# Merging the third and fourth key tile of a head into one exponential, and one masking product for two heads

## What is computed

```
x = x + attention(wkv(x, fside, fside, w1, u1, cond), w_qkv, w_o)
x = x + ffn(wkv(x, fside, fside, w2, u2, cond), w_gate, w_up, w_down)
```

## Time and profile before

| | |
|---|---|
| median of 3 runs | 988.72 us (987.49 to 988.75) |
| the profiled execution | 986.6 us, span 984.6 us |
| PE, matmuls | 728.8 us busy, 74% of the span |
| DVE | 785.0 us, 80% |
| ACT | 473.8 us, 48% |
| ACT's exponentials of attention (L499) | 256, 99.9 us |
| PE's key scores (L1198, L1199, L1200) | 3 x 256 products |
| PE's masks by query (L1176) | 256 products |
| granted TensorE clock, mean | 0.948 |

### The profile page before, as it was taken

One profiled execution on the slowest core, in us unless ns is written; L12 is line 12 of the kernel. 1 busy time (PEld: TensorE's weight loads), 2 busy tenths in 40 slices (PEclk: granted clock), 3 DMA queues, 4 the chain that ended last, 5 costly groups with the idle time before them and its releaser, 6 DMA issues.

```text
span 984.6 us, 10348 instructions
## 1 busy us (share of the span) xinstructions
PE 728.8 (74%) x3761; PEld 361.3 (37%) x3761; DVE 785.0 (80%) x1064; ACT 473.8 (48%) x758; POOL 73.6 (7%) x149
## 2 busy tenths in 40 slices
PE   0110107769878999897889998978899989987656
PEld 0000003334544444444444444444444444653222
DVE  3999999977997878879978788799787886534566
ACT  5645644336675353356753532567535324452230
POOL 1000000111100001111000011110000111100000
PEclk9999999799899999999979999999899998999788
DMA  8612210254400002744000027440000273400001
GB/s 319 235 43 96 96 53 11 66 126 128 109 22 22 1 12 61 206 130 106 22 22 1 11 52 211 124 116 23 22 0 11 53 204 73 100 1 1 1 0 43
DMA packets 30305, 72.23 MB, mean 73 GB/s; under 512 B 5808, under 2 KB 5808, under 8 KB 28464
## 3 DMA queue, kind: packets, MB, share of 16 engines
q1 hardware_dynamic: 19792, 46.94, 15.9%
q0 software_dynamic: 6144, 16.79, 7.2%
q10 hardware_dynamic: 4320, 7.87, 2.3%
HBM read 33.82 MB, written 4.19 MB: 39 GB/s over the span
## 4 chain that ended last, share of the span: by engine, by line
PE 45%; DVE 33%; issue 10%; ACT 8%; DMA 3%; SPq 1%; POOL 0%; DVEq 0%; ACTq 0%
PE bank L1285 12%; PE bank L1148 6%; PE bank L1297 5%; PE bank L1225 4%; PE bank L1214 4%; PE bank L1141 4%; PE bank L1198 4%; ACT region L499 3%; PE bank L1174 3%; DVE negmax L953 2%; DMA stacks<-rows 2%; PE bank L1199 2%; DVE num L853 2%; DVE region L772 2%; DVE fn L839 2%
## 5 line engine op out<-in xcount | busy, mean ns | idle before, releaser
L953 DVE TENSOR_REDUCE negmax<-bank 128x4 f32<-128x512 f32 (+2 forms) x96 | 99.3, 1035 | 52.3 <-PE bank L1176 52.3
L1198 PE MATMUL bank<-stacks 128*128 128x512 f32 (+3 forms) x256 | 108.7, 426 | 35.1 <-ACT region L499 32.2
L499 ACT ACTIVATE region<-bank 128x512 f32<-128x512 f32 (+3 forms) x256 | 99.9, 433 | 64.3 <-PE bank L1200 64.1
L296 POOL DMA_DIRECT2D stacks<-rows x128 | 69.5, 550 | 780.4 <-DVE region L741 361.2
L1148 PE MATMUL bank<-h,wqkv 128*128 128x512 f32 x256 | 116.1, 604 | 7.4 <-DVE region L1105 4.2
L1174 PE MATMUL bank<-stacks 128*128 128x128 f32 (+3 forms) x256 | 85.2, 414 | 9.0 <-DVE negmax L953 4.7
L1199 PE MATMUL bank<-maxrow,pick 128*128 128x512 bf16 (+3 forms) x256 | 83.6, 326 | 0.0
L1141 PE MATMUL bank<-wqkv,h 128*128 128x512 f32 x128 | 70.1, 705 | 16.0 <-ACT rows L487 16.0
L1198 PEld LDWEIGHTS bank<-stacks 128*128 128x128 f32 x256 | 51.5, 201 | 67.2 <-ACT region L499 51.9
L1307 PE MATMUL bank<-identb,region 128*128 128x128 bf16 x36 | 5.5, 307 | 95.3 <-DVE region L749 63.6
L1285 PE MATMUL bank<-region,gate_q 128*128 128x512 bf16 x256 | 62.2, 387 | 16.8 <-DVE region L741 16.8
(11 more groups left out here) (150 smaller groups left out, 1378.8 us busy)
## 6 DMA issues: line engine op xcount, KB each, us to landing
stacks<-rows SPq DMA_DIRECT2D x128, 128.0 KB, 4.0
stacks<-rows POOLq DMA_DIRECT2D x128, 128.0 KB, 4.3
kt<-in_fside ACTq DMA_DIRECT2D x30, 256.0 KB, 3.1
h<-in_x SPq DMA_DIRECT2D x4, 1024.0 KB, 5.7
region<-in_w_gate SPq DMA_DIRECT2D x4, 1024.0 KB, 12.1
xt<-in_x SPq DMA_DIRECT2D x4, 1024.0 KB, 7.3
region<-in_w_up SPq DMA_DIRECT2D x4, 1024.0 KB, 5.5
region<-in_w_down SPq DMA_DIRECT2D x4, 1024.0 KB, 4.6
```

The source lines that it names most:

```text
L296: eng.dma_start(stacks[HD * r:HD * r + HD, at:at + 2, i, :].bitcast(F32), rows[mine, q:k + 1:k - q, :]).then_inc(stacked[s][i], 16)
L499: nc.scalar.activation(probs[:, i, P_AT[t]:P_AT[t] + CAUSAL[t]], bank[4 + n % 2][:, 0:CAUSAL[t]], ACT.Exp, scale=SCALE).then_inc(p_ready, 1)
L953: nc.vector.tensor_reduce(o, scored, AX_X, ALU.max, negate=True).then_inc(max_taken, 1)
L1198: nc.tensor.matmul(o, ks[s][:, i, P * t:P * t + P], qs[s][:, i, P * t:T], start=True, stop=False)
```

## The change

Key tiles 2 and 3 of a head (256 and 128 columns) go into one bank side by side, as one unit with six products and one exponential of 384 columns. A group has 12 units instead of 16. In `scores`, the first two query tiles, where two heads share a bank, get one masking product for both: `hide_qk` is read twice by a step of zero, and the output is two strips of 128 columns. The unit numbers in ACT's order, in the waits of the stacks and in `SLOT_BEHIND` are put in the new count.

```diff
+    KEY_TILES = ((0,), (1,), (2, 3))
+    PER_HEAD = len(KEY_TILES)
+    UNITS = HG * PER_HEAD
...
                 if g >= 2:
-                    eng.wait_ge(st_ready, b * (GROUPS * UNITS) + (g - 2) * UNITS + TT * (i + 1))
+                    eng.wait_ge(st_ready, b * (GROUPS * UNITS) + (g - 2) * UNITS + PER_HEAD * (i + 1))
...
-                    nc.scalar.activation(probs[:, i, P_AT[t]:P_AT[t] + CAUSAL[t]],
-                                         bank[4 + n % 2][:, 0:CAUSAL[t]], ACT.Exp,
+                    nc.scalar.activation(probs[:, i, P_AT[tiles[0]]:P_AT[tiles[0]] + columns],
+                                         bank[4 + n % 2][:, 0:columns], ACT.Exp,
                                          scale=SCALE).then_inc(p_ready, 1)
...
-                exps(b, 0, 0, 6)
+                exps(b, 0, 0, 5)
                 cap_exp(b, 4)
-                exps(b, 0, 6, 10)
+                exps(b, 0, 5, 8)
                 load_k(b, 3)
                 reciprocals(b, 3)
                 own_exp(b, 4)
-                exps(b, 0, 10, 16)
+                exps(b, 0, 8, 12)
...
-                    mm = nc.tensor.matmul(o[:, c + P * t:c + w], identb[:, :], hide_qk[:, :],
-                                          start=False, stop=True, skip_group_check=True)
+                    if t >= 2:
+                        mm = nc.tensor.matmul(o[:, P * t:w], identb[:, :], hide_qk[:, :],
+                                              start=False, stop=True, skip_group_check=True)
+                    elif i % 2:
+                        pair = o[:, 0:2 * w].rearrange("p (i w) -> p i w", i=2)[:, :, P * t:w]
+                        mm = nc.tensor.matmul(pair, identb[:, :], hide_qk[:, :].rearrange("p (o w) -> p o w", o=1).to_broadcast([P, 2, P]),
+                                              start=False, stop=True, skip_group_check=True)
...
-                o = bank[4 + n % 2][:, 0:CAUSAL[t]]
-                nc.tensor.matmul(o, ks[s][:, i, P * t:P * t + P], qs[s][:, i, P * t:T], start=True, stop=False)
-                nc.tensor.matmul(o, pick[:, i, :], maxrow[:, s, P * t:T], start=False, stop=False)
-                nc.tensor.matmul(o[:, 0:P], identb[:, :], hide_kq[:, :], start=False, stop=True).then_inc(st_ready, 1)
+                for t in tiles:
+                    c = P_AT[t] - P_AT[tiles[0]]
+                    o = bank[4 + n % 2][:, c:c + CAUSAL[t]]
+                    nc.tensor.matmul(o, ks[s][:, i, P * t:P * t + P], qs[s][:, i, P * t:T],
+                                     start=True, stop=False, skip_group_check=True)
+                    nc.tensor.matmul(o, pick[:, i, :], maxrow[:, s, P * t:T], start=False, stop=False, skip_group_check=True)
+                    mm = nc.tensor.matmul(o[:, 0:P], identb[:, :], hide_kq[:, :], start=False, stop=True, skip_group_check=True)
+                mm.then_inc(st_ready, 1)
...
-                        if g == 0 and n == 9:
+                        if g == 0 and n == 7:
                             project_values(b, 1)
...
-SLOT_BEHIND = ({1: 0, 3: 1, 6: 2, 9: 3, 12: 4, 15: 5}, {3: 2, 7: 3, 11: 4, 15: 5})
+SLOT_BEHIND = ({1: 0, 2: 1, 4: 2, 7: 3, 9: 4, 11: 5}, {2: 2, 5: 3, 8: 4, 11: 5})
```

More of the change, by code:

```diff
@@ L56, in adaln_attention_ffn @@
     P_LEN = sum(CAUSAL)
-    UNITS = HG * TT
+    KEY_TILES = ((0,), (1,), (2, 3))
+    PER_HEAD = len(KEY_TILES)
+    UNITS = HG * PER_HEAD
     SLOTS = 6
@@ L496, in exps @@
                 for n in range(first, last):
-                    i, t = n // TT, n % TT
+                    i, tiles = n // PER_HEAD, KEY_TILES[n % PER_HEAD]
+                    columns = sum(CAUSAL[t] for t in tiles)
                     act.wait_ge(st_ready, b * (GROUPS * UNITS) + g * UNITS + n + 1)
-                    nc.scalar.activation(probs[:, i, P_AT[t]:P_AT[t] + CAUSAL[t]],
-                                         bank[4 + n % 2][:, 0:CAUSAL[t]], ACT.Exp,
+                    nc.scalar.activation(probs[:, i, P_AT[tiles[0]]:P_AT[tiles[0]] + columns],
+                                         bank[4 + n % 2][:, 0:columns], ACT.Exp,
                                          scale=SCALE).then_inc(p_ready, 1)
@@ L548, in turn @@
                 sum_reciprocal(b, 0)
-                exps(b, 1, 0, 4)
+                exps(b, 1, 0, 3)
                 load_k(b, 4)
@@ L553, in turn @@
                 own_exp(b, 5)
-                exps(b, 1, 4, 12)
+                exps(b, 1, 3, 9)
                 weigh(b, 5, 0)
                 weigh(b, 5, 1)
-                exps(b, 1, 12, 16)
+                exps(b, 1, 9, 12)
                 cap_exp(b, 6)
@@ L563, in turn @@
                 sum_reciprocal(b, 1)
-                exps(b, 2, 0, 4)
+                exps(b, 2, 0, 3)
                 weigh(b, 6, 0)
                 weigh(b, 6, 1)
-                exps(b, 2, 4, 12)
+                exps(b, 2, 3, 9)
                 cap_exp(b, 7)
-                exps(b, 2, 12, 16)
+                exps(b, 2, 9, 12)
                 load_k(b, 6)
@@ L578, in turn @@
                 weigh(b, 7, 1)
-                exps(b, 3, 0, 6)
+                exps(b, 3, 0, 5)
                 cap_exp(b, 8)
-                exps(b, 3, 6, 12)
+                exps(b, 3, 5, 9)
                 load_k(b, 7)
@@ L584, in turn @@
                 own_exp(b, 8)
-                exps(b, 3, 12, 16)
+                exps(b, 3, 9, 12)
                 weigh(b, 8, 0)
@@ L1188, in scores_by_key @@
             def scores_by_key(b, g, n):
-                s, i, t = g % 2, n // TT, n % TT
+                s, i, tiles = g % 2, n // PER_HEAD, KEY_TILES[n % PER_HEAD]
                 if n == 0:
```

## The result

| | before | after |
|---|---|---|
| median | 988.25 us (987.49 to 988.75, 4 runs) | 977.40 us (976.17 to 978.02, 4 runs) |
| ratio | 1 | 0.9889, 95% interval 0.9872 to 0.9906 |
| the profiled execution | 986.6 us, span 984.6 | 977.25 us, span 975.5 |
| granted TensorE clock, mean | 0.948 | 0.955 |

The change wins 10.85 us. A second measurement of the same kernel at another time gave 978.34 us against 989.08, ratio 0.9893 (0.9878 to 0.9909).

What follows compares the result with a forecast made beforehand. PE was taken to lead group 0, DVE then through group 2 in b0 to b2, PE and ACT alternating in group 3. Terms 1.25 + 1.5 + 1.0 + 1.2 + 0.1 + 0.3 = 5.35 us off median 988.72 gave 983.4; range 978.8 to 987.4.

Steps and rivals of the forecast that it cites:

- The masks: One masking product for two in 64 places, about 20 pairs on the path: 0.3 us gained, bounds -2.0 to +1.8.
- Group 3 of b3: Last batch, last attention group: three heads gain 0.48 us each from fewer bank exchanges, the last head loses; 1.25 us gained.
- Group 0 of b3: Last batch, first attention group: PE's three stops for exponentials shrink to one of 0.2 us; 1.0 us gained.
- groups 1 and 2: Middle attention groups: DVE covers any gain in the first three batches; the last batch gains 0.1 us in all.
- Group 0 of b0 to b2: First group, first three batches: POOL issues stacks earlier but full DMA limits landing; 0.4 us a batch, 1.2 us gained.
- Group 3 of b0 to b2: Last group, first three batches: exponentials finish sooner, then ACT's reciprocals wait for DVE's sum; 1.5 us gained.
- The rival of the slower side: Longer PE idle in group 3 of b0 to b2 lowers the clock through `weigh_values`: 3.65 us slower, 992.4; chance 0.08.
- The stacks follow POOL: Issue, not full DMA engines, sets stack landing; group 0 of b0 to b2 gains 1.05 us each; 980.3 us, chance 0.2.
- The gains stay under cover: DVE takes back all gains in b0 to b2, only b3's remain; 986.4 us, chance 0.17.

Runs made afterwards that it cites:

- experiment 3: The whole change, but each pair's mask is two products of 128 columns again, both behind the two scores; 980.95 us, ratio 0.9917.
- experiment 5: The whole change, but the pair mask only in query scores of groups 0 and 1; groups 2 and 3 mask each head separately; 981.53 us, ratio 0.9921.
- experiment 6: A quarter of x loaded for the next batch instead of all, in the whole change (972.50 us) and in the kernel before (984.73 us).
- experiment 7: With a quarter of x loaded for the next batch: merged units with old masks, 976.80 us; pair masks with old units, 979.10 us.
- experiment 2: The kernel before with only the pair masks added; 983.96 us, ratio 0.9949.
- experiment 1: The whole change with the masks of the kernel before, so merged units and new order only; 985.39 us, ratio 0.9961.

## Why the prediction was too low

**The masks, 0.3 us forecast: the step that failed.** "Nearest is the row with equal columns, 0": I took a product's own start-to-start time, 0.04 us, for what its removal is worth, and capped the saving at 0.09 a pair by an equal share. Measured are 0.08 a pair in the first tile, just under that cap, and 0.13 in the second, above it, and for the masks alone 5.1 us. The price was wrong twice. Nearly half of it (0.18 of 0.41 us) is not the product taken out but the two scores that now follow each other (experiment 3), and a row that shows a mask's start says nothing of what it costs the score behind it. And the number of pairs on the path was not 20: b3's 12, group 0's 12 more in b0 to b2, those ahead of `project_values`, and, if experiment 5 is more than noise, those of groups 2 and 3 in b0 to b2. Rows count 3.2 us; the other 1.9 can lie in b0 to b2 or in the noise, and are not told apart, since a single profile scatters there by as much. The upper bound of the term, 1.8, lay below even the lower end of what it measured (3.5), and with it the range ended above the time.

**Group 3 of b3, 1.25.** Its own terms make 1.28 (three times 0.48, less 2.11 - 1.95 = 0.16). Measured 1.16. Exponentials of t=0 come 2.07 us apart (forecast 2.03):

```profile
870.31 1.75 ACT L502 ACTIVATE region<-bank 128x384 f32<-128x384 f32 x3 [0.52 <-PE bank L1211]
872.38 1.74 ACT L502 ACTIVATE region<-bank 128x384 f32<-128x384 f32 x3 [0.32 <-PE bank L1211]
874.45 1.74 ACT L502 ACTIVATE region<-bank 128x384 f32<-128x384 f32 x3 [0.32 <-PE bank L1211]
```

**Group 0 of b3, 1.0, and groups 1 and 2, 0.1.** Merged units alone: 0.89 and 0.22. Each is within 0.12 us.

**Group 0 of b0 to b2, 1.2.** The view was right: landing leads, and PE's stop grew. But PE starts the first query scores of group 2 only 0.6 us earlier in three batches together, masks included, in either profile of the change. The profiles give 1.2 to 1.4 us for groups 0 to 2 together, masks included. Experiments 6 and 7 show what the landing costs: 1.30 us a batch is there (0.9 of the merged units, 0.4 of the masks) and is mostly taken back. That 1.2 came out near is luck: the masks brought it, and with the merged units alone the same groups were 4.5 us longer in the one profile there is, a slow one in which the stop was longer and slow stretches followed.

**Group 3 of b0 to b2, 1.5.** The reciprocals start 0.43 us after DVE's sum (forecast 0.4):

```profile
497.72 0.63 ACT L436 ACTIVATE rec<-den 128x512 f32<-128x512 f32 x1 [0.43 <-DVE den L867]
```

The stage gave 2.4 to 4.0 us. Its length goes by how much of the slow clock falls there: 20.73, 22.24 and 22.05 before, 20.53, 20.18 and 20.28 after, 20.24, 21.77 and 20.60 in its repetition. Over all sixteen profiles it takes 20.2 to 20.8 us with 3.4 us at 1.2 GHz and 21.1 to 22.2 with 6.8 or 10.2. The closest pair is that of experiment 7, where every batch had 3.4 us: 20.59, 20.56 and 20.60 with the merged units, 20.80, 20.61 and 20.63 with the old ones, 0.3 us for the three. Taken over all kernels, 36 batches with merged units average 20.9 us and 12 with the old ones 21.5, which would be 1.8 for three batches. So the units themselves are worth little there, and the 1.5 came near by slow stretches that fell elsewhere; whether the merged units move those is not shown.

**The clock.** The rival of the slower side did not come. PE's stop in group 3 of b0 did grow, as it said, but `weigh_values` there took 6.13 us (second fence, from the chain) against 5.99:

```profile
305.61 0.38 PE L1208 MATMUL bank<-stacks 128*128 128x256 f32 x1 [2.89 <-ACT region L502]
```

```profile
307.09 6.13 PE bank L1226 x64
```

And the mean granted clock rose, from 0.944 in 57 runs of before to 0.952 in 8 of the change, about 16 us less at 1.2 GHz (twice the missing share of the time). Across the 57 runs of before, 0.001 more goes with 0.27 us less (0.16 to 0.34 in its four groups of runs); in the runs of experiments 2, 3 and 5 it is 0.35 to 0.38, in those of experiment 1 0.65. By all but the last, 1 to 3 of the 10.85 us come with the clock. This is a correlation, and what moves the stretches is not settled. The Trainium skill (TensorE: Matmul & The Clock Gate, What's actually happening) says that one and the same kernel has differing numbers of its first matmuls at the slow level from run to run. No run here shows that start; in mid-kernel the place of the slow stretches differs between the two profiles of the change, 29.4 and 31.6 us behind the copy in b2.

**The rivals.** *The stacks follow POOL* came nearest in time, 980.3, for the wrong reason: POOL issued the last stack 1.5 us earlier and it landed 0.8 us earlier at best, 0.9 later in b0. *The gains stay under cover* fell, since outside b3 the two profiles of the change won 5.6 and 5.1 us.

None of the experiments beats the change; those with a quarter of the load leave work out. What is left in it is about 5 us at the landing (experiment 6, an upper estimate, since less was loaded there), for whoever finds another time for the next batch's load.

## What to carry to other kernels

The price of a small product on PE is read from a run of its neighbours, start of the first score to start of the next with and without it, not from its own row. Before an earlier issue is booked as a gain, look at what else moves bytes then: a quarter of the load in a throwaway variant tells in one run what the landing costs. A slot of work that waits for another engine must not stand ahead of work that a third engine has queued for.

## What was not expected of the hardware

Two masking products of 128 columns, each behind its score product (fp32 data, stacked rows), replaced by one of 256 behind both scores: that saves 0.08 us a pair when the scores have 128 columns and 0.13 when they have 256, though a mask's own start-to-start time reads 0.04. Regrouping alone, with as many products, gives nearly half of it (0.18 of 0.41 us a group).

The last of eight stacks of 128 KB takes 3.0 to 3.8 us from issue to landing beside a 256 KB load, and 5.3 to 7.2 us beside one of 1 MB (the change, b0 to b2); issued by SP's queue, which then makes the last four, it takes 5.1 to 5.4 us.

A stop of PE of 1.6 to 3.5 us at one place was followed in 15 of 23 batches by 3.4 or 6.8 us at a granted clock of 0.50, a shorter one or none in 1 of 25. Idle products of 1.5 to 2.2 us in the stop kept the clock at 1.00 there in all six batches; whether that helps the whole depends on where the next slow stretch falls.
